# Attention scores in two half-row passes with the parts of the keys kept twice, in a two-layer gated cross-attention kernel

## What is computed

```python
q = split_heads(layernorm(x) @ Wq + bq)            # (4, 16, 512, 16)
k, v = split_heads(ctx @ Wk + bk), split_heads(ctx @ Wv + bv)
scores = einsum('bhqd,bhkd->bhqk', q, k) / sqrt(16)
scores = scores + bias        # layer 0: a bias per head and a key mask per sequence
                              # layer 1: one mask for all heads and sequences
out = einsum('bhqk,bhkd->bhqd', softmax(scores), v)
x = x + tanh(g_xattn[layer]) * (out_in_tokens @ Wo + bo)
```

## Time and profile before

| | |
|---|---|
| median of 3 runs (lowest to highest) | 996.31 us (994.21 to 996.57) |
| the profiled execution | 998.35 us |
| its span, first to last instruction | 996.6 us |
| mean granted TensorE clock, share of full | 0.977 |
| busy: PE, DVE, POOL, ACT | 94%, 58%, 57%, 50% |
| first and last scores matmul of layer 0 and 1 together | 61.98 and 648.9 us |
| one load of q or k (192 KB), issue to landing, median | 3.3 and 3.9 us |

### The profile page before, as it was taken

One profiled execution on the slowest core, in us unless ns is written; L12 is line 12 of the kernel. 1 busy time (PEld: TensorE's weight loads), 2 busy tenths in 40 slices (PEclk: granted clock), 3 DMA queues, 4 the chain that ended last, 5 costly groups with the idle time before them and its releaser, 6 DMA issues. The chain is left out here.

```text
span 996.6 us, 21412 instructions
## 1 busy us (share of the span) xinstructions
PE 941.2 (94%) x7733; PEld 535.7 (54%) x7734; DVE 582.7 (58%) x1716; ACT 494.1 (50%) x676; POOL 572.7 (57%) x611
## 2 busy tenths in 40 slices
PE   6979999999989999989999999997899999999994
PEld 3544444444467444544444444465456677777753
DVE  4868888888828444568888888837442222222227
ACT  2438778777845233337887778744111122222210
POOL 3449999999957611149999999951046122222210
PEclk9979999999989999979999999999999999999998
DMA  9563837364143332325353524131812112122153
GB/s 304 194 213 63 234 66 223 77 178 102 22 138 100 119 95 67 88 85 118 66 119 65 116 49 106 34 89 51 297 59 85 61 59 63 59 64 64 53 165 109
DMA packets 96910, 107.56 MB, mean 108 GB/s; under 512 B 15690, under 2 KB 80722, under 8 KB 96818
## 3 DMA queue, kind: packets, MB, share of 16 engines
q1 hardware_dynamic: 86498, 88.30, 32.4%
q10 hardware_dynamic: 6912, 8.65, 2.8%
q0 software_dynamic: 3408, 9.38, 2.6%
HBM read 76.92 MB, written 29.38 MB: 107 GB/s over the span
## 5 line engine op out<-in xcount | busy, mean ns | idle before, releaser
L636 ACT ACTIVATE pT<-ps 128x1024 f32<-128x1024 f32 x256 | 248.6, 1023 | 85.8 <-PE ps L510 85.5
L674 POOL TENSOR_TENSOR xT<-nmax,xT 128x512 f32<-128x512 f32 x192 | 195.7, 1041 | 22.4 <-DVE nmax L578 22.3
L674 POOL TENSOR_TENSOR s<-nmax,s 128x512 f32<-128x512 f32 x188 | 192.6, 1041 | 22.4 <-DVE nmax L578 18.1
L578 DVE CUSTOM_DVE_ANT_0 s<-ps,bias 128x512 f32<-128x512 f32 x256 | 166.1, 688 | 41.1 <-PE ps L497 39.9
L578 DVE CUSTOM_DVE_ANT_0 xT<-ps,bias 128x512 f32<-128x512 f32 x256 | 166.5, 689 | 39.2 <-PE ps L497 33.5
L497 PE MATMUL ps<-ks,qs 97*128 97x512 bf16 (+1 forms) x512 | 162.3, 398 | 10.0 <-PEq L156 4.8
L525 PE MATMUL ps<-pT,vq 128*32 128x512 f32 x1024 | 135.1, 604 | 2.5
L1571 POOL DMA_INDIRECT slots_out<-y,id x39 | 38.2, 980 | 130.1 <-DVE y L1898 130.1
L497 PEld LDWEIGHTS ps<-ks,qs 97*128 97x128 bf16 (+1 forms) x512 | 30.7, 98 | 130.3 <-DVE nmax L578 64.5
L1650 PE MATMUL ps<-gu,xgT 128*128 x312 | 98.8, 460 | 0.7 <-ACT xgT L1734 0.7
L510 PEld LDWEIGHTS ps<-ident,xT 64*128 64x128 f32 x2048 | 69.4, 139 | 28.1 <-issue 27.8
(11 more groups left out here) (203 smaller groups left out, 1210.8 us busy)
## 6 DMA issues: line engine op xcount, KB each, us to landing
bias<-in_bias SPq DMA_DIRECT2D x14, 1024.0 KB, 6.0
qk_scratch<-parts SPq DMA_DIRECT2D x64, 128.0 KB
qs<-qk_scratch SPq DMA_DIRECT2D x32, 192.0 KB, 3.3
ks<-qk_scratch SPq DMA_DIRECT2D x32, 192.0 KB, 3.9
gu<-in_gate_up SPq DMA_DIRECT2D x8, 704.0 KB, 9.4
slots_in<-zeros SPq DMA_DIRECT2D x4, 1280.0 KB, 7.5
xg<-slots_in SPq DMA_DIRECT2D x39, 130.0 KB, 2.1
qk_scratch<-parts ACTq DMA_DIRECT2D x32, 128.0 KB
```

The source lines that it names most:

```text
L578: nc.vector.tensor_tensor_reduce(at.s[m % 4][:, qt, :], sb.ps[:, ring_bank(tile_place[u - 1 + hg * 64]), :], at.bias[:, j if per_head_bias ...
L636: nc.scalar.activation(at.pT[:, slot(m // HG, m % HG), 2 * half:2 * half + 2, :], sb.ps[:, 2 + 2 * half:4 + 2 * half, :], ACT.Exp).then_in ...
L674: nc.gpsimd.tensor_tensor(s, at.nmax[:, m % 4, qt:qt + 1].to_broadcast([P, S]), s, ALU.subtract).then_inc(pool_less_max, 1)
```

## The change

The six products are spread over two passes of 48 rows. `RUNS` is now a list of (pass, row, parts): pass 0 has the run of three, pass 1 the run of two and the run of one. In layer 0 the ones and the key mask take row 32 of pass 1, and the last run moves down by one row, so that pass 1 has 49 rows. `qs` keeps query tiles 0 and 1 in the lower half of the rows (0 to 63) and 2 and 3 in the upper one; `ks` is held in both halves, for both passes. `scores` takes two query tiles at once, one from each half: pass 0 of both, then pass 1 of both, which accumulates in the same bank. So the tiles come in the order 0, 2, 1, 3 (`Q_ORDER`), and DVE, ACT and POOL take them in that order. The wait for a bank stands before the first pass of each tile. A load has four DMAs per run in place of two, and two for the key mask in place of one; queries come in pieces of 256 columns (512 B) instead of 512. The maximum is subtracted with the same split between ACT and POOL (their functions change like `add_bias` and are left out below).

```diff
@@ -37,8 +37,10 @@
 NEG = -1.0e30
 MASK_C = -1000000000.0
 
-RUNS = [(0, 3), (3, 2), (5, 1)]
-KS = DH * 6
+PASSES = 2
+RUNS = [(0, 0, 3), (1, 0, 2), (1, 2 * DH, 1)]
+KS = 2 * DH
+Q_ORDER = (0, 2, 1, 3)
 PARTS = 8
 STORED = 48 * (4 * B // PARTS)
 EARLY = 2
@@ -107,15 +109,19 @@
 
 def load_qk(eng, at, dram, per_head_bias, hg, b):
 
-    for start, count in RUNS:
-        rows = slice(start * DH, (start + count) * DH)
-        for which, dst, first in ((0, at.qs, 3 - count), (1, at.ks, 0)):
-            src = dram.qk[which, :, first:first + count, :, b * S:(b + 1) * S].rearrange(
-                "(g j) s d t -> g (s d) j t", j=HG)
-            eng.dma_start(dst[rows, b % 2, :, :], src[bass.ds(hg, 1)].rearrange("g p j t -> (g p) j t")
+    for pas, row, count in RUNS:
+        row += 1 if per_head_bias and row == KS else 0
+        for half in range(2):
+            rows = slice(half * HP + row, half * HP + row + count * DH)
+            queries = slice(b * S + half * S // 2, b * S + (half + 1) * S // 2)
+            src = dram.qk[0, :, 3 - count:3, :, queries].rearrange("(g j) s d t -> g (s d) j t", j=HG)
+            eng.dma_start(at.qs[rows, b % 2, pas, :, :], src[bass.ds(hg, 1)].rearrange("g p j t -> (g p) j t")
                           ).then_inc(at.qk_loaded[b % 2], 16)
-    if per_head_bias:
-        eng.dma_start(at.ks[KS:KS + 1, b % 2, :, :],
+            src = dram.qk[1, :, 0:count, :, b * S:(b + 1) * S].rearrange("(g j) s d t -> g (s d) j t", j=HG)
+            eng.dma_start(at.ks[rows, b % 2, pas, :, :], src[bass.ds(hg, 1)].rearrange("g p j t -> (g p) j t")
+                          ).then_inc(at.qk_loaded[b % 2], 16)
+    for half in range(2 if per_head_bias else 0):
+        eng.dma_start(at.ks[half * HP + KS:half * HP + KS + 1, b % 2, PASSES - 1, :, :],
                       dram.keymask[b:b + 1, :].unsqueeze(1).to_broadcast([1, HG, S])
                       ).then_inc(at.qk_loaded[b % 2], 16)
 
@@ -182,7 +188,10 @@
                                         base=0, pattern=[[-1, P]], channel_multiplier=1).then_inc(consts, 1)
                 pool.wait_ge(consts, 2)
 
-                nc.gpsimd.memset(at.qs[KS:KS + 1, :, :, :], 1.0).then_inc(consts, 1)
+                for half in range(2):
+                    ones = at.qs[half * HP + KS:half * HP + KS + 1, :, PASSES - 1, :, :]
+                    fill = nc.gpsimd.memset(ones, 1.0)
+                fill.then_inc(consts, 1)
                 pool.wait_ge(consts, 3)
             else:
                 pool.nop().then_inc(consts, 3)
@@ -396,8 +405,8 @@
 
 
     per_head_bias = bias_dram is not None
-    K = KS + 1 if per_head_bias else KS
-    LOADS = 2 * len(RUNS) + (1 if per_head_bias else 0)
+    KEPT = [3 * DH, 3 * DH + 1 if per_head_bias else 3 * DH]
+    LOADS = 4 * len(RUNS) + (2 if per_head_bias else 0)
     qk_loaded, bias_loaded = at.qk_loaded, at.bias_loaded
     scores_done = sem(tag + "scores_done")
     biased = sem(tag + "biased")
@@ -486,16 +495,25 @@
         def _(pe):
             pe.nop().then_inc(scores_done, 32)
 
-            def scores(hg, m, qts):
+            def scores(hg, m, first_place):
+
                 b, j = m % M // HG, m % HG
-                for qt in qts:
-                    if j == 0 and qt == 0:
-                        pe.wait_ge(qk_loaded[b % 2], (hg * 2 + (m // HG) // 2 + 1) * (16 * LOADS))
-                    place = tile_place[hg * 64 + 4 * m + qt]
-                    if place >= 3:
-                        pe.wait_ge(*ring[place - 3])
-                    nc.tensor.matmul(sb.ps[:, ring_bank(place), :], at.qs[0:K, b % 2, j, qt * P:(qt + 1) * P],
-                                     at.ks[0:K, b % 2, j, :], start=True, stop=True).then_inc(scores_done, 1)
+                for pas in range(PASSES):
+                    for i in range(2):
+                        k = first_place + i
+                        if pas == 0:
+                            if j == 0 and k == 0:
+                                pe.wait_ge(qk_loaded[b % 2], (hg * 2 + (m // HG) // 2 + 1) * (16 * LOADS))
+                            place = tile_place[hg * 64 + 4 * m + k]
+                            if place >= 3:
+                                pe.wait_ge(*ring[place - 3])
+                        half, col = divmod(Q_ORDER[k] * P, S // 2)
+                        rows = slice(half * HP, half * HP + KEPT[pas])
+                        last = nc.tensor.matmul(sb.ps[:, ring_bank(tile_place[hg * 64 + 4 * m + k]), :],
+                                                at.qs[rows, b % 2, pas, j, col:col + P], at.ks[rows, b % 2, pas, j, :],
+                                                start=(pas == 0), stop=(pas == PASSES - 1))
+                        if pas == PASSES - 1:
+                            last.then_inc(scores_done, 1)
 
             def turn(hg, m):
 
@@ -536,8 +554,9 @@
                                                sb.ident[:, :])
                 last.then_inc(out_turned, 1)
 
-            scores(0, 0, range(QT))
-            scores(0, 1, range(QT))
+            for m in range(2):
+                scores(0, m, 0)
+                scores(0, m, 2)
 
             def body(hg, first, last):
                 for m in range(M):
@@ -546,12 +565,12 @@
                     if not (first and b == 0):
                         values(*before(hg, b), j)
                     if ahead:
-                        scores(hg, m + 2, (0, 1))
+                        scores(hg, m + 2, 0)
                     if j == 0 and not (first and b < 2):
                         turn_out(*before(*before(hg, b)))
                     turn(hg, m)
                     if ahead:
-                        scores(hg, m + 2, (2, 3))
+                        scores(hg, m + 2, 2)
                 if last:
                     turn_out(hg, B - 2)
                     for kt in range(QT):
@@ -564,15 +583,15 @@
             dve.nop().then_inc(biased, 2)
             dve.nop().then_inc(out_done, 1)
 
-            def add_bias(hg, m, qts):
+            def add_bias(hg, m, places):
 
                 b, j = m % M // HG, m % HG
-                for qt in qts:
-                    u = 4 * m + qt + 1
-                    if per_head_bias and b == 0 and qt == 0:
+                for k in places:
+                    u, qt = 4 * m + k + 1, Q_ORDER[k]
+                    if per_head_bias and b == 0 and k == 0:
                         dve.wait_ge(bias_loaded[j], (hg + (m // M + 1)) * 16)
                     dve.wait_ge(scores_done, hg * 64 + (u + 32))
-                    if qt == 0:
+                    if k == 0:
                         dve.wait_ge(turned, (hg * M + m) * 2 + 2)
                     dve.sem_inc(granted, 1)
                     nc.vector.tensor_tensor_reduce(
...
@@ -1982,8 +2003,8 @@
 
             sb.v = made("v", [P, TT, D], F32)
             at.bias = made("bias", [P, HG if layer == 0 else 1, QT, S], F32)
-            at.qs = made("qs", [P, 2, HG, S], BF16)
-            at.ks = made("ks", [P, 2, HG, S], BF16)
+            at.qs = made("qs", [P, 2, PASSES, HG, S // 2], BF16)
+            at.ks = made("ks", [P, 2, PASSES, HG, S], BF16)
             at.vq = made("vq", [P, 2, QT, HG, VW], F32)
 
         def projection_buffers(made):
```

More of the change, by code:

```diff
@@ L624, in _, with subtract_max @@
             act.nop().then_inc(out_kept, 1)
-            def subtract_max(hg, m, qts):
-                for qt in qts:
-                    act.wait_ge(biased, hg * 64 + 4 * m + qt + 1 + 2)
+            def subtract_max(hg, m, places):
+                for k in places:
+                    qt = Q_ORDER[k]
+                    act.wait_ge(biased, hg * 64 + 4 * m + k + 1 + 2)
                     s = at.s[m % 4][:, qt, :]
@@ L667, in _, with subtract_max @@
             pool.nop().then_inc(out_turned, 1)
-            def subtract_max(hg, m, qts):
-                for qt in qts:
-                    pool.wait_ge(biased, hg * 64 + 4 * m + qt + 1 + 2)
+            def subtract_max(hg, m, places):
+                for k in places:
+                    qt = Q_ORDER[k]
+                    pool.wait_ge(biased, hg * 64 + 4 * m + k + 1 + 2)
                     s = at.s[m % 4][:, qt, :]
```

## The result

The changed kernel takes **1002.48 us** (median of 10 runs, 998.04 to 1007.63) beside 995.32 us for the kernel before on the same chip: ratio 1.0076, interval 1.0049 to 1.0103. It is slower by 5 to 10 us, where no change was forecast. The ten fall into two groups, five at 998.0 to 1000.5 us with a mean granted clock of 0.972 to 0.979 and five at 1004.5 to 1007.6 with 0.966 to 0.972. The profiled execution took 1006.06 us and is of the upper group, 3.6 us above the median, with a span of 1004.3; the span of before is 996.6, in an execution 3.0 us above its median. The two traces are compared here by those spans, +7.7 us.

The account below looks back on a forecast made before the run. PE's order of work was taken to bound the steady part, with POOL next. Terms -9.6 + 0.6 + 6 + 2.5 + 0.3 = -0.2 us, set on the 996.31 median, gave 996.1 us, range 984 to 1007.

Parts of the forecast that it names:

- Part 1, the passes: Scores matmuls: four half-row matmuls per pair of query tiles, two at a time, take 0.44 us, as now.
- Part 2, the changes of form: PE between scores and transposes: both now half-row, saving 0.29 and 0.37 us; output's turn costs 0.10; sum 0.47 per batch.
- Part 3, the wait for the bank: Second tile of a pair waits 0.08 us for its bank in two plain heads; saving becomes 0.32 per batch.
- -9.6: Attention batches: total saving in us, from 0.32 per batch over 30 batches.
- partly behind other waits: Each layer's first eight tiles, paced by DVE: pair cycle some 0.3 us longer, partly hidden; +0.3 a layer, at most +1.
- Part 4, the loads: Loads 2.8 us longer, hidden in plain batches; waits of 2.3, 1.2 and 2.5 at layer 0's head-group changes, +6 us.
- time goes by packets more than by bytes: Batch loads: 2 KB packets take 86 ns, hardly more than 1 KB ones; hence 2.8 us added per load.
- Part 5, the start of layer 0: Projection block's end: seven more SP issues cost +5.2, stores give back up to 3.4; +2.5, plus +0.3 for second load.
- The loads stay hidden: Rival on batch loads: half packets cost half and late stores find DMA free; 984 to 990 us; chance 0.27.
- The loads decide: Slower rival: 3.9 us more per load, waits 4.4, 3.3 and 4.6, SP takes 5; about 1006 us; chance 0.15.
- The second pass's weights are not hidden: Slower rival in scores: pass 2's weight reload exposed by 0.10 us per pair, +25, about 1020 us; chance 0.08.
- The halves do not run together: Slower rival in scores: row halves do not overlap, 0.43 us more per pair, +110, near 1105 us; chance 0.03.

Follow-up runs that it names:

- the keys once: Changed kernel, but after a layer's first two batches key parts and mask row go to the lower half of the rows only: 997.04 us, ratio 0.9996.
- experiment 5: Changed kernel with later loads bringing keys to the lower half only (997.04 us, ratio 0.9996), or queries to the lower half only (995.19 us, 0.9979).
- experiment 3: Kernel before with each load DMA split in two: 996.01 us, ratio 1.0005; changed kernel with later loads for the lower half only: 993.84, 0.9998.
- The first experiment: Both kernels with parts loaded for a layer's first two batches only, biases once: before 998.26 us, ratio 1.0017; changed 994.45, ratio 0.9999.
- experiment 6: Changed kernel with the first load's upper half issued by ACT: 998.37 us, ratio 1.0043; also bias 0 between the next group's load halves: 999.18, 1.0057.

## Why the prediction was wrong

The mechanisms of the forecast were nearly all seen; their sum was -0.2 us and the result is +7.6 by the ratio. The terms below are as the one profiled execution of each kernel has them.

*Part 1, the passes, 0.44 per pair:* right. The matmuls of a pass start 3 to 4 ns apart, the second pass 0.226 us after the first.

*Part 2, the changes of form:* right in kind. Scores to transposes gives 0.09 to 0.10, as forecast. Transposes to scores fell by 0.15 in plain heads, not 0.09: 0.54 per batch instead of 0.37. The turn costs 0.10 before it, as forecast, and 0.05 more after it.

*Part 3, the wait for the bank:* in the second pair of a head the second tile starts 0.13 to 0.15 us behind the first, in three heads of four, where 0.08 in two was forecast. From there to values the four heads take 0.13, 0.10, 0.02 and 0.15 longer than before (the 0.10 in the head whose values wait for exp): 0.39 per batch, where the forecast had 0.08 x 2 + 0.09 = 0.25. Net the batch gained 0.29 against 0.32. But the **-9.6** took 30 batches; 14 of a layer run so, and the ends of each layer are 0.4 longer: 14 x 0.29 - 0.4 = 3.6 per layer, **-7.2**. The start was the worse miss: a pair there takes 1.56 us (67.20 to 68.76) instead of 2 x 0.61, and 0.34 times nearly four pairs is +1.3 a layer. The text had the 0.3 per pair and then called it "partly behind other waits"; nothing hides it, as DVE paces that stretch. **+2.6 instead of +0.6**, beyond its end of +1 a layer. Together the passes give 4.6 us where 9.0 were forecast.

*Part 4, the loads:* the waits were forecast as 2.3, 1.2 and 2.5 and came as 3.5, 0.6 and 2.9: **+7.0 instead of +6**. That the size was near is in part luck. The forecast counted the engines' time alone, 2.8 us more per load. A plain load of the changed kernel takes 0.52 x 9.0 = 4.7 us of the 16 engines, two others 5.0 and 5.9, where three of the kernel before take 4.0 to 4.2; the addition is 1.1 on average:

```profile
90.10:99.10 9.00, 8.96 (x131) 4.35 (x132) 7.45 (x23) 7.09 (x9) 9.00 (x11) 1.00 0.52 134
```

So "time goes by packets more than by bytes" was wrong for these packets, as the keys once show too (experiment 5). What made up for it was left out: twice as many issues took 1 to 3 us of the margin by themselves (experiment 3). Also left out, and priced at nothing without a reason, is the clock: **+3.6 instead of 0** in the profiled execution.

*Part 5, the start of layer 0:* **+3.3 instead of +2.8**, with +1.4 to +2.8 in six later profiles of the same start: right. Seven more issues took 3.7 us, not 5.2, and the last stores gave back less; with the old form's packets in as many DMAs the cost was 0.8 (experiment 3). Layer 1 lost nothing, as forecast.

The terms as measured: -7.2 + 2.6 + 7.0 + 3.6 + 3.3 = 9.3; less 1.0 for the clock in layer 1's start, and less 0.5 between the layers that stays unexplained, that is the span's +7.7 but for rounding. **Two steps failed, by about as much.** Part 4 priced a late load by its wait alone: 10.6 us instead of 6, of which 3.6 are the stretches at half the clock behind waits of 2.3 and 3.1 us. Part 3 had the gain of the passes twice too large: 4.6 us instead of 9.0, by the paced start of each layer, the longer waits for the bank, and 30 batches where 28 run steadily. The first experiment shows the second miss by itself: with no load late the kernel is level with the one before, where the forecast's own terms without Part 4's make 6.2 us less.

That the late loads make the loss is shown without the trace as well: six kernels of the new form in which no load is late by more than 0.3 us stand at ratios of 0.998 to 1.000, the changed one at 1.0076. How that splits into waits and clock is read from one execution; without the 3.6 the terms make 5.7 us, within the 4.9 to 10.3 of the ratio's interval, so the clock's share in the median is not shown.

*The rivals.* "The loads stay hidden", the likeliest of them at 0.27, is refuted by the three waits. "The loads decide" (1006) named the right mechanism and sign, 0.15 was too little for it; its own waits, 4.4, 3.3 and 4.6, were too long. "The second pass's weights are not hidden" is refuted: the second pass starts 0.226 us after the first. Its weights go to rows that the first still streams through; here the four loads of two passes are done at 542.33, 0.11 us after the first pass began, and the second begins at 542.45 (timelines of PEld and of PE to 542.44):

```profile
542.22 0.11 PEld L512 LDWEIGHTS ps<-ks,qs 48*128 48x128 bf16 x4 [0.84 <-DVE nmax L597]
...
542.22 0.39 PE L512 MATMUL ps<-ks,qs 48*128 48x512 bf16 x2
```

The Trainium skill, "TensorE: Matmul & The Clock Gate", section "The mechanism", says in its list of what overlaps that a weight load overlaps running matmuls only where its row group differs; this trace disagrees. The section's first paragraph also names a background weight buffer, and by that the overlap would be allowed. "The halves do not run together" is refuted by the 3 to 4 ns between the two matmuls of a pass.

## What to carry to other kernels

Where a load stands beside other transfers, set its margin (here 2 to 3 us) against both what the change adds in DMA issues and what it adds in data; either alone may fit where both do not. Once a load is late, look at the granted clock behind the wait too, and charge it where it falls. Price the stretch in which another engine sets the pace by that engine's cycle, not by PE's. And put such a change where the loads have room: here layer 1, whose loads meet no biases, kept the gain that layer 0 gave back.

## What the runs showed of the hardware

The granted clock fell to 0.50 beside four PE waits for a load: of 3.1 us (ended at 133.6) and 2.3 (at 245.2) in the changed kernel, and in the two kernels of experiment 6 of 3.4 (at 240.8) and 2.7 (at 238.3), for 6.8, 3.4, 6.8 and 3.4 us. It began between 1.0 us ahead of the wait's end and 1.0 behind it. Beside the shorter waits for a load, 0.2 to 1.2 us, it stayed at 1.00, and in the kernels without late loads it did not fall in that stretch. That falls and longer waits stand together is what the records show; what the chip goes by is not.

The stretch at half the clock where layer 0's attention begins was not the same length in all profiled runs: 10.2 us in the kernel before, 13.7 in the changed one, 27.3 with the keys once, where the first four heads are 4.17, 4.18, 4.17 and 4.62 us instead of 3.97, 2.79, 2.80 and 3.43. That is 4.2 us, as much as most of the effects here; so lengths of layers are compared head by head, and totals by the ratios.
